# A decoder layer on one core: the queries' way through DRAM, the conv taps' buffers, the order of SyncE's list and of one copy

## The reference

```python
mixed = jax.nn.silu(_causal_conv1d(hidden_states @ w_qkv, conv_w))   # 4 taps a channel
q, k, v = jnp.split(mixed, [KDIM, 2 * KDIM], axis=-1)
q = _l2norm(q); k = _l2norm(k)
...
def step(St, inp):                       # for each token
    St = St * jnp.exp(g_t)[..., None, None]
    v_old = jnp.einsum('bhk,bhkv->bhv', k_t, St)
    delta = (v_t - v_old) * b_t[..., None]
    St = St + k_t[..., None] * delta[:, :, None, :]
    o = jnp.einsum('bhk,bhkv->bhv', q_t, St)
...
core = core * rsqrt(mean(core * core) + EPS) * norm_weight * silu(z)
return core @ w_out
```

## Time and profile before

| | |
|---|---|
| median of three runs | 3450.14 us (3445.16 to 3451.03) |
| profiled execution, its own time | 3444.88 us |
| its span, first to last instruction | 3443.1 us |
| granted TensorE clock, mean | 0.98 |
| busy share of the span: PE, DVE, ACT, POOL | 94%, 67%, 48%, 56% |
| one slot of `delta_rule`, shortest | 36.33 us |

### The profile page before, as it was taken

How to read it: one execution, slowest core, us unless ns; L and a number is a source line. 1 busy time by engine, 2 the same in 40 slices (tenths; PEclk the granted TensorE clock), 3 DMA queues, 4 the chain that set the end, 5 groups by cost and what they waited for, 6 DMA issues and landing times. The chain is left out here.

```text
span 3443.1 us, 59910 instructions
## 1 busy us (share of the span) xinstructions
PE 3236.4 (94%) x20064; PEld 2115.5 (61%) x20064; DVE 2300.1 (67%) x3494; ACT 1666.4 (48%) x5111; POOL 1920.2 (56%) x1888
## 2 busy tenths in 40 slices
PE   5899999999999999998999999999988999999999
PEld 2567666676667666676667666676763444454444
DVE  6788788887888788787878787787870000024453
ACT  2456566565656566565656565565662000011232
POOL 2677677777777677776767677776760000001032
PEclk8999999999999999999999999999999999999999
DMA  2233333333333333333333333333334222211001
GB/s 98 57 79 94 88 83 84 88 88 87 81 82 91 90 82 85 84 86 93 78 83 84 83 96 84 84 77 98 82 96 173 98 106 89 98 37 61 1 13 37
DMA packets 469200, 282.30 MB, mean 82 GB/s; under 512 B 311808, under 2 KB 410240, under 8 KB 463360
## 3 DMA queue, kind: packets, MB, share of 16 engines
q1 hardware_dynamic: 467600, 271.39, 29.6%
q10 hardware_dynamic: 1296, 7.09, 0.5%
HBM read 173.17 MB, written 88.34 MB: 76 GB/s over the span
## 5 line engine op out<-in xcount | busy, mean ns | idle before, releaser
L762 PE MATMUL acc<-xT,wc 128*128 128x512 f32 x2048 | 944.0, 605 | 9.2 <-DVE d_kks L1092 7.2
L1019 DVE SCALAR_TENSOR_TENSOR d_conv<-acc,wc,d_conv 128x511 f32<-128x511 f32 (+2 forms) x768 | 566.1, 737 | 94.0 <-ACT d_conv L1198 82.4
L762 PEld LDWEIGHTS acc<-xT,wc 128*128 128x128 f32 x2048 | 375.0, 193 | 384.3 <-issue 383.7
L775 PE MATMUL acc<-wc,xT 128*128 128x256 f32 x2048 | 473.4, 385 | 0.0
L1058 DVE STREAM_TRANSPOSE d_em<-d_dm 128x1024 f16<-128x1024 f16 x256 | 314.6, 1229 | 196.0 <-ACT d_dm L1249 195.9
L775 PEld LDWEIGHTS acc<-wc,xT 128*128 128x128 f32 x2048 | 379.8, 190 | 45.6
L1249 ACT ACTIVATE d_dm<-acc 128x512 f16<-128x512 f32 x384 | 227.2, 592 | 233.4 <-PE acc L820 233.3
L1546 PE MATMUL acc<-t_area 128*128 128x512 f32 x768 | 332.5, 593 | 2.2 <-ACT t_area L1995 2.2
L1065 DVE CAST_PREDICATED d_zm<-cons,d_tz 128x512 f16<-128x512 int32 x384 | 264.1, 688 | 90.6 <-PE d_tz L807 84.0
L1198 ACT ACTIVATE d_conv<-acc,wc 128x512 f32<-128x512 f32 x256 | 175.1, 684 | 300.0 <-PE acc L762 176.3
L2052 POOL TENSOR_SCALAR t_veps<-t_mv 128x1 f32<-128x1 f32 x32 | 9.7, 303 | 546.8 <-DVE t_mv L1791 546.8
(11 more groups left out here) (226 smaller groups left out, 6951.1 us busy)
## 6 DMA issues: line engine op xcount, KB each, us to landing
d_decay<-decay_rows SPq DMA_DIRECT2D x64, 512.0 KB, 5.1
v_rows<-d_vb SPq DMA_DIRECT2D x256, 128.0 KB, 2.8
d_vn<-v_rows SPq DMA_DIRECT2D x64, 512.0 KB, 3.7
core_rows<-d_ob SPq DMA_DIRECT2D x1024, 32.0 KB, 1.7
t_area<-core_rows SPq DMA_DIRECT2D x30, 1024.0 KB, 4.8
wc<-in_w SPq DMA_DIRECT2D x96, 256.0 KB, 3.0
k_rows<-d_kf SPq DMA_DIRECT2D x256, 64.0 KB, 3.9
d_kn<-k_rows SPq DMA_DIRECT2D x64, 256.0 KB, 2.9
```

The lines of the kernel that those rows point to most:

```text
L762: last = nc.tensor.matmul(bank(TILE[j])[:, :], wtile(j, k), xT[:, k, r % B * S:(r % B + 1) * S], start=k == 0, stop=k == KT - 1)
L775: last = nc.tensor.matmul(bank(f"z{j}")[:, i * GV * P:(i + 1) * GV * P].rearrange("p (h n) -> p h n", h=GV), xT[:, k, r % B * S + (2 * j + ...
L1019: nc.vector.scalar_tensor_tensor(c[:, d:S], bank(TILE[j])[:, 0:S - d], tap(j, KS - 1 - d), c[:, d:S], ALU.mult, ALU.add).then_inc(taps, 1)
```

## The change

1. **Taps.** They get a tile `taps2` with two places, used in turn by the groups. The load of a group's taps no longer waits for the last conv step of the group before, but for that of the group before that one (one group earlier). Its place, in the slot where the last batch of the old group is m, is the same.
2. **Queries.** `move_q` becomes `store_q`, four stores of 64 KB to a new DRAM tensor `q_rows`, and `load_q`, one load of 256 KB.
3. **SP's list.** A slot now begins with `store_q(n-2)`, `store_o(n-4)`, `load_q(n-2)`. Then come the weights of queries and keys and the taps, as before. The weights of one value head move behind `load_k`.
4. **Squares.** `o_square` writes its squares over `qf`, as bf16. It waits until the queries of iteration s+1 have been stored, and `flip_q(m)` waits for the squares of m-2. The wait of `o_square` for `stored`, and that of `flip_o` for the squares, go away.
5. **First output.** ScalarE does `first_output(s)` ahead of `o_scale(f)` and `k_square(n)`.

```diff
-MOVED = 16 * NC * NC
+MOVED = 16 * (NC + 1)
+SENT = 16 * NC
-            return wc[:, WCOLS + j * KS + k:WCOLS + j * KS + k + 1]
+            return taps2[:, (n[0] * (ROUND // B) + n[1] // B) % 2, j * KS + k:j * KS + k + 1]
...
             def slot(n, project, invert, recur, finish):
+                if recur:
+                    store_q(back(n, 2))
+                if finish:
+                    store_o(back(n, 4))
+                if recur:
+                    load_q(back(n, 2))
                 if invert:
                     next_weights(back(n, 1), 1)
                 if project:
                     next_weights(n, 0)
                 if invert:
                     next_weights(back(n, 1), TILES)
-                if recur:
-                    move_q(back(n, 2))
-                if project:
-                    next_weights(n, 3)
                 if n[0] * ROUND + n[1] < ITERS - 1:
                     load_decay((n[0], n[1] + 1))
                 if project:
                     store_k(n)
                     load_k(n)
+                    next_weights(n, 3)
...
-                if finish:
-                    store_o(back(n, 3))
...
-                        sp.wait_ge(taps, at(n, 12, 12))
+                        wait(sp, taps, at(back(n, B), 12, 12))
...
-            def move_q(m):
+            def store_q(m):
                 sp.wait_ge(v_flipped, at(m, 2, 2))
+                wait(sp, q_moved, at(back(m, 1), MOVED, MOVED))
+                for a in range(NC):
+                    sp.dma_start(q_dram[m[1] % 2].rearrange("b i a n -> a i b n")[a],
+                                 qf[a * 32:(a + 1) * 32].rearrange("p b c j -> p b (c j)")).then_inc(q_moved, 16)
+
+            def load_q(m):
+                sp.wait_ge(q_moved, at(m, MOVED, SENT))
                 wait(sp, q_squares, at(back(m, 1), NC, NC))
-                for a in range(NC):
-                    for b in range(NC):
-                        sp.dma_start(qn[b * 32:(b + 1) * 32, a].rearrange("p c j -> p (c j)"),
-                                     qf[a * 32:(a + 1) * 32, b].rearrange("p c j -> p (c j)")).then_inc(q_moved, 16)
+                sp.dma_start(qn[:, :, :, :].rearrange("p a c j -> p (a c j)"),
+                             q_dram[m[1] % 2].rearrange("b i a n -> (b i) (a n)")).then_inc(q_moved, 16)
...
             def flip_q(m):
                 dve.wait_ge(silued, nth(m, "silued", 1))
-                wait(dve, q_moved, at(back(m, 1), MOVED, MOVED))
+                wait(dve, o_squares, at(back(m, 2), GV * NC, GV * NC))
+                wait(dve, q_moved, at(back(m, 1), MOVED, SENT))
...
-                if (c, h) in ((1, 0), (0, 1)):
-                    out = junk[:, h, :]
-                else:
-                    wait(act, stored, at(back(s, 1), STORES, STORES))
-                    out = ob[:, c, h * NC:(h + 1) * NC, :].rearrange("p b j -> p (b j)")
+                if s[0] * ROUND + s[1] < ITERS - 1:
+                    act.wait_ge(q_moved, at(back(s, -1), MOVED, SENT))
+                out = squared[:, h * NC + c, :]
...
                 if invert:
                     copy_d(m, 1)
+                if recur:
+                    first_output(s)
                 if finish:
                     o_scale(f, 0)
                     o_scale(f, 1)
                 if project:
                     k_square(n)
-                if recur:
-                    first_output(s)
```

More of the change, by code:

```diff
@@ L30 @@
 GCOLS = WCOLS + 4 * KS
+TAPS = 4 * KS
 LEVELS = 6
@@ L111, in bc, with head @@
     return ap.unsqueeze(axis).to_broadcast(shape)
-def head(nc, a, xT, tabs, cons, nw, wc, w_loaded, taps_loaded):
+def head(nc, a, xT, tabs, cons, nw, wc, taps2, w_loaded, taps_loaded):
     with ExitStack() as ctx:
@@ L152, in _ @@
                 cols = slice(j * KT * P, (j + 1) * KT * P) if j < TILES else slice(WCOLS, GCOLS)
-                sp.dma_start(wc[:, cols], a["w"][0, :, cols]).then_inc(w_loaded[j] if j < TILES else taps_loaded, 16)
+                dst = wc[:, cols] if j < TILES else taps2[:, 0, :]
+                sp.dma_start(dst, a["w"][0, :, cols]).then_inc(w_loaded[j] if j < TILES else taps_loaded, 16)
             sp.wait_ge(rows_ready, B)
@@ L317, in _, with delta_rule @@
                 nc.scalar.activation(spread(Q_CDEC, b), gathered(pss[2], b), ACT.Exp).then_inc(act_chain, 1)
-def delta_rule(nc, xT, tabs, cons, nw, wc, w_loaded, taps_loaded, acc, early_loaded, early_weighed, decay_dram, w_dram, k_dram, v_dram, core_dram, wout):
+def delta_rule(nc, xT, tabs, cons, nw, wc, taps2, w_loaded, taps_loaded, acc, early_loaded, early_weighed, decay_dram, w_dram, k_dram, q_dram, v_dram, core_dram, wout):
     with ExitStack() as ctx:
@@ L343, in delta_rule @@
         oo = many("oo", 2, [P, GV, NC, P])
-        junk, kqs, kks = sb("junk", [P, GV, P], BF16), sb("kqs", [P, S]), sb("kks", [P, S])
+        kqs, kks = sb("kqs", [P, S]), sb("kks", [P, S])
         kss, qss, rkt, rk = sb("kss", [P, NC]), sb("qss", [P, NC]), sb("rkt", [P, NC]), many("rk", 2, [P, 2, NC])
         qf, qn = sb("qf", [P, NC, NC, 32]), sb("qn", [P, NC, NC, 32])
+        squared = qf[:, :, :, :].rearrange("p b c j -> p (b c j)").bitcast(BF16).rearrange("p (n d) -> p n d", d=P)
         eq = many("eq", 4, [P, NC])
@@ L394, in wtile, with tap @@
             return wc[:, (j * KT + k) * P:(j * KT + k + 1) * P]
-        def tap(j, k):
-            return wc[:, WCOLS + j * KS + k:WCOLS + j * KS + k + 1]
+        def tap(n, j, k):
+            return taps2[:, (n[0] * (ROUND // B) + n[1] // B) % 2, j * KS + k:j * KS + k + 1]
         def tab(n, q, h=None, c=None):
@@ L480, in load_weights @@
                 src = w_dram[g, :, cols] if isinstance(g, int) else w_dram[bass.ds(g, 1), :, cols].rearrange("a p n -> (a p) n")
-                sp.dma_start(wc[:, cols], src).then_inc(w_loaded[j] if j < TILES else taps_loaded, 16)
+                dst = wc[:, cols] if j < TILES else taps2[:, g % 2, :]
+                sp.dma_start(dst, src).then_inc(w_loaded[j] if j < TILES else taps_loaded, 16)
             def load_decay(n):
@@ L588, in _ @@
             for u in range(ITERS):
-                slot((u // ROUND, u % ROUND), True, u >= 1, u >= 2, u >= 3)
+                slot((u // ROUND, u % ROUND), True, u >= 1, u >= 2, u >= 4)
             slot((ROUNDS, 0), False, True, True, True)
@@ L592, in _ @@
             slot((ROUNDS, 2), False, False, False, True)
+            slot((ROUNDS, 3), False, False, False, True)
             sp.wait_ge(stored, STORES * ITERS)
@@ L1018, in convolve @@
                     dve.wait_ge(taps, nth(n, "taps", 3 * j + d - 2))
-                nc.vector.scalar_tensor_tensor(c[:, d:S], bank(TILE[j])[:, 0:S - d], tap(j, KS - 1 - d),
+                nc.vector.scalar_tensor_tensor(c[:, d:S], bank(TILE[j])[:, 0:S - d], tap(n, j, KS - 1 - d),
                                                c[:, d:S], ALU.mult, ALU.add).then_inc(taps, 1)
@@ L1048, in flip_o @@
                 wait(dve, stored, at(back(s, 1), STORES, STORES))
-                dve.wait_ge(o_squares, at(s, GV * NC, GV * NC))
                 nc.vector.transpose(ob[:, :, :, :], oo[s[1] % 2][:, :, :, :].rearrange("p h c (a j) -> p a (h c) j", a=NC)).then_inc(o_flipped, 1)
@@ L1197, in first_tap @@
                 free(act, n, TILE[j], CONV_ORDER, CONV_BUFFER, SILUED, CONV_LAG)
-                nc.scalar.activation(conv_of(TILE[j])[:, :], bank(TILE[j])[:, :], ACT.Copy, scale=tap(j, KS - 1)).then_inc(tap0, 1)
+                nc.scalar.activation(conv_of(TILE[j])[:, :], bank(TILE[j])[:, :], ACT.Copy, scale=tap(n, j, KS - 1)).then_inc(tap0, 1)
             def silu(n, j):
@@ L2091, in decoder_layer @@
         with ExitStack() as ctx:
-            tabs, wc = (ctx.enter_context(nc.sbuf_tensor(n, s, F32)) for n, s in (("tabs", [P, G, B, QN * GV * NC]), ("wc", [P, GCOLS])))
-            head(nc, a, xT, tabs, cons, nw, wc, w_loaded, taps_loaded)
+            tabs, wc, taps2 = (ctx.enter_context(nc.sbuf_tensor(n, s, F32)) for n, s in (("tabs", [P, G, B, QN * GV * NC]), ("wc", [P, WCOLS]), ("taps2", [P, 2, TAPS])))
+            head(nc, a, xT, tabs, cons, nw, wc, taps2, w_loaded, taps_loaded)
             acc = [outer.enter_context(nc.psum_tensor(f"acc{i}", [P, S], F32)) for i in range(4)]
-            delta_rule(nc, xT, tabs, cons, nw, wc, w_loaded, taps_loaded, acc, early_loaded, early_weighed, a["decay"], a["w"], a["k_rows"], a["v_rows"], a["core"], a["wout"])
+            delta_rule(nc, xT, tabs, cons, nw, wc, taps2, w_loaded, taps_loaded, acc, early_loaded, early_weighed, a["decay"], a["w"], a["k_rows"], a["q_rows"], a["v_rows"], a["core"], a["wout"])
         tail(nc, a, cons, nw, xT, acc)
@@ L2138 @@
     args["k_rows"] = nc.dram_tensor("k_rows", (2, NC, 32, NC, S // NC), F32, kind="Internal").ap()
+    args["q_rows"] = nc.dram_tensor("q_rows", (2, NC, 32, NC, S // NC), F32, kind="Internal").ap()
     args["v_rows"] = nc.dram_tensor("v_rows", (2, NC, 32, NC, GV * S // NC), F32, kind="Internal").ap()
```

## The result

The changed kernel takes 3468.04 us (median of 4 runs, 3466.22 to 3468.91). The kernel before took 3450.59 us in the same comparison. The ratio is 1.005, with a 95% interval from 1.0033 to 1.0068: slower by half a per cent, where 3464 us was forecast.

What follows compares the result with a forecast made beforehand. TensorE's own work was taken to set the slot at 36.33 us, leaving 153.3 us to win. Taps +71 and ordinary slots -57, squares and ends 0, gave +14 on 3450.1: 3464 us, range 3441 to 3506.

Steps and rivals of the forecast that it cites:

- The taps' term, +71: In the 15 first slots of a group, taps issued 4.75 us later lengthen TensorE's wait by that much each: +71 us.
- I take no more clock loss than now: In the first slots, TensorE's longer standstill was to cost no further time at half clock: 0 us added.
- a restart had one price: On TensorE, a restart's clock cost was to hang on the work after it, not the standstill's length; sum stays 71.
- The case with more half clock, +98: Rival: first slots each lose 1.8 us more to half clock, 27 us more, 3491 us in all; chance 0.14.
- What would show it: List of signs after the change, among them first_tap waiting about 12 us for the taps in each of 15 first slots.
- SyncE through with the first three entries at F + 10.5: SyncE's slot list: four query stores, 16 output stores and one load done about 10.5 us after flip_q ends (F).
- The ordinary slots, -57: The 44 other slots were to lose all they hold above 36.33 us each, 56.9 us, with the late keys' waits.
- Both cures act on the same 56.9 us, and either would do.: In the 44 other slots, the first output's earlier copy or the sooner keys would each win the 56.9 us.
- what is queued behind the late keys is then copy_d(m, 2): On ScalarE, with the first output's copy moved ahead, copy_d(m, 2) stands behind k_square, so late keys could still hurt.
- The squares' wait, 0: Ordinary slots: query stores land in some 3.4 us, within o_square's cover of F + 4.3, so nothing is lost.
- a sign of DRAM's price: Trace rows, direct transfers 1.8 us against key stores 3.9, read as agreeing with the rule that HBM is the slowest target.
- Ends, 0: Last slots: o_square's old waits for stores go, new ones for queries of up to 3.4 us come; 0, bounds -4 and +4.

Runs made afterwards that it cites:

- experiment 1: The changed kernel with the taps' load moved first in SyncE's slot list, ahead of the query stores: 3293.83 us, ratio 0.9546 to the kernel before.
- experiment 3: The changed kernel with the output stores in two halves of 8 and the taps' load between them: 3374.92 us, ratio 0.977 to the kernel before.
- experiment 4: The kernel before with two tap buffers and the weaker wait, every entry of SyncE's list where it was: 3454.07 us, ratio 1.0006.
- experiment 6: The changed kernel with the first output's copy back behind o_scale and k_square: 3464.29 us, ratio 1.0039 to the kernel before.
- experiment 7: The kernel before with only the first output's copy moved ahead of o_scale and k_square: 3439.47 us, ratio 0.9966.
- experiment 8: The kernel before with decay, key stores and key load ahead of the 16 direct query transfers in SyncE's list: 3401.31 us, ratio 0.9841.
- experiment 10: The changed kernel with the output stores ahead of the query stores in SyncE's list: 3699.62 us, ratio 1.0726 to the kernel before.
- experiment 9: The kernel before with two tap buffers, taps loaded a slot earlier, and decay and keys ahead of the 16 direct query transfers: 3296.34 us, ratio 0.955.
- experiment 2: The changed kernel with the taps' load between the query stores and the output stores: 3295.96 us, ratio 0.955 to the kernel before.

## Why the prediction was right, and where it was not

**The taps' term, +71, measured +78.** The mechanism and its place are shown three ways: by the row at F + 10.7, by experiment 1, which removes all of it with one moved entry, and by the points of experiment 3. That the second buffer is worth nothing by itself is shown by experiment 4.

The size was off by 0.45 us a slot, and the step that failed is "I take no more clock loss than now". TensorE's wait grew from 4.1 to 8.6 us on average, 4.5, and all its idle time in a first slot (length less busy time) by 4.3, a little less than the 4.75 forecast. Its busy time at the same work, beyond the 36.23 of an ordinary slot, grew from 2.1 to 3.0 us, where nothing was forecast: 4.3 + 0.9 = 5.2, times 15 the 78. Two stretches after the standstill shown above:

```profile
1157.20:1160.70 3.50, 3.50 (x22) 2.85 (x23) 3.15 (x6) 2.78 (x7) 1.62 (x2) 0.50 0.15 50
1160.70:1164.10 3.40, 3.40 (x8) 1.53 (x6) 2.93 (x5) 1.72 (x7) 3.40 (x4) 0.62 0.44 137
```

In the kernel before, two stretches after the standstill of 3.5 us, and the stretch behind the one at the stage's end:

```profile
1145.58:1149.10 3.52, 3.52 (x22) 2.85 (x23) 2.91 (x5) 2.83 (x7) 1.52 (x2) 0.52 0.11 28
1149.10:1152.60 3.50, 3.50 (x12) 1.53 (x10) 3.29 (x5) 1.79 (x7) 3.50 (x4) 1.00 0.13 33
...
2620.30:2625.00 4.70, 4.70 (x12) 2.10 (x11) 0.00 (x0) 0.00 (x0) 0.00 (x0) 1.00 1.00 424
```

At 0.50 and 0.62 the levels 1.2 and 2.4 GHz give 3.5 and 2.6 us at half clock, 3.0 us of work lost. After the 3.5 us of before, 1.7 were lost, and at the stage's end, after 9.4 us of idle and so the longest of the three, 1.6. The rule of the Trainium skill (TensorE: Matmul & The Clock Gate, "What's actually happening") was read there as if a restart had one price. These rows show that it had not, and that the length of the standstill does not order the prices either; what sets them stays open. The case with more half clock, +98, was too high as well.

Two slips of the prediction change nothing in its sum. "What would show it" puts first_tap's wait at about 12 us, where its own numbers give 8.2 + 4.75 = 13.0; measured are 12.8. And it has SyncE through with the first three entries at F + 10.5, where its terms add to F + 10.1; measured is F + 10.2.

**The ordinary slots, -57, measured -56.4.** The size was right, since it was all that a slot could lose, but one step of its reasoning was wrong: "Both cures act on the same 56.9 us, and either would do." Experiments 6, 7 and 8 show that SyncE's order does it alone (56.6 us in these slots) and is not helped by the copy's place, while the copy's place alone makes the kernel 12 us faster. The size came out right although that step was wrong, because the other cure was in the change as well. The prediction had written down why ("what is queued behind the late keys is then copy_d(m, 2)") and did not ask when TensorE needs that copy: 0.6 us after the one that was cured (in experiment 7, read_q starts at 1121.06 and the idle time before level_z at 1121.66).

**The squares' wait, 0, measured 0.** From 200 to 2519 us o_square waits 4.5 us in all for the query stores, at most 1.0 at a time, and no ordinary slot is longer for it. The DMA issues of the changed kernel (KB each, median us to landing), key stores and query stores:

```profile
k_rows<-d_kf SPq DMA_DIRECT2D x256, 64.0 KB, 3.5
...
q_rows<-d_qf SPq DMA_DIRECT2D x256, 64.0 KB, 1.8
```

Stores of one size and form land in 1.8 us with no large load ahead and in 3.5 right behind the decay load. Experiment 8 shows the same for the key stores themselves, which in its list leave 3 to 4 us after the decay load and not right behind it:

```profile
k_rows<-d_kf SPq DMA_DIRECT2D x256, 64.0 KB, 1.8
```

The 64 KB stores to DRAM land as soon as the direct transfers of 16 KB did, so the 3.9 against 1.8 us in which the prediction saw a sign of DRAM's price came from the load right ahead. The Trainium skill's rule on the write receipt (DMA: Bandwidth & Descriptors, "Anatomy of one DMA"), that HBM is the heaviest target, stands in a section on transfers that GpSimd issues; SyncE issues these, and no run here shows such a price for them. The cover is thin all the same: experiment 10 delays these stores by 5.5 us and loses 232.

**Ends, 0.** The spans' difference, 21.3, is that of the 59 slots, 21.6. In the last slots o_square waits for the query stores, 3.0 us at most, as foreseen. The queries' load and the moved value weights show no wait.

That the five transfers themselves are worth nothing was implied by the prediction and is shown by experiment 9.

## What to carry to other kernels

A second buffer shortened nothing here as long as the load that fills it stood at the same place of an in-order issuing list. Ask first whether the removed wait was met when the issuer came to it, then what stands ahead of the load now, and put the load that another engine stands for ahead of everything that waits. When a copy is moved out from behind a late transfer, look for what becomes the first thing behind it and when that is needed; curing the lateness was worth more here (55 us) than reordering its victims (12). Price a list by the distance from the event that starts it to each issue: that distance gave the first slots of the changed kernel and of experiments 2, 3 and 10 to within 1.3 us.

## What the runs showed of the hardware that I had not expected

- Four 64 KB stores to DRAM landed in 1.8 us each (median), the same as the direct SBUF transfers of 16 KB before. The key stores of the same size took 3.9 us right behind the decay load of 512 KB (the kernel before) and 1.8 when they left 3 to 4 us after it (experiment 8).
- The 8 KB load of the taps landed 1.9 us after issue with output stores right ahead (experiment 3) and 2.8 us with two 256 KB weight loads right ahead (the kernel before).
- After a standstill of 8.4 us TensorE ran 3.5 us at 0.50 and the next 3.4 at 0.62 of its clock (the changed kernel); after one of 3.5 us, at the same place of the slot, 3.5 us at 0.52 and the next 3.5 at 1.00; after one of 9.4 us at the stage's end 3.4 us at 0.52 and the next 4.7 at 1.00 (both the kernel before).
